# Routed-expert tiles of an FFN: list loads moved from SyncE's to ScalarE's DMA queue, and the weighting moved to the end of ScalarE's step

## The reference, cut to what matters

```python
y = cond_ref(x, ...)                          # 8192 tokens of 512, dense
shared = silu(xf @ sh_gate_w) * (xf @ sh_up_w) @ sh_down_w
topk_idx, w = _route(xf, router_w, e_bias)    # 8 of 64 experts for each token
order = argsort(topk_idx.reshape(-1)); tok = order // 8
g = ragged_dot(xf[tok], gate_w, group_sizes)  # 512 -> 256, by expert
u = ragged_dot(xf[tok], up_w, group_sizes)
o = ragged_dot(silu(g) * u, down_w, group_sizes) * w[order]
routed = zeros.at[tok].add(o)                 # out = x + shared + routed
```

## Time and profile before

| | us |
|---|---|
| median of 3 runs (4018.2 to 4027.15) | 4022.19 |
| the profiled execution, its own time | 3993.73 |
| span of the profiled execution | 3992.0 |
| routed part, from the first `e_sg` to the last | 2522.7 |
| PE busy in the span | 3867.9 (97%) |
| ACT busy in the span | 1444.0 (36%) |
| mean granted TensorE clock | 0.986 |

### The profile page before, as it was taken

One profiled execution on the slowest core, in us unless ns is written; L12 is line 12 of the kernel. 1 busy time (PEld: TensorE's weight loads), 2 busy tenths in 40 slices (PEclk: granted clock), 3 DMA queues, 4 the chain that ended last, 5 costly groups with the idle time before them and its releaser, 6 DMA issues.

```text
span 3992.0 us, 90448 instructions
## 1 busy us (share of the span) xinstructions
PE 3867.9 (97%) x19160; PEld 3180.6 (80%) x19161; DVE 1654.4 (41%) x3528; ACT 1444.0 (36%) x2807; POOL 1916.5 (48%) x1598
## 2 busy tenths in 40 slices
PE   6999999999999969999999999999999999999997
PEld 5888888888888758888888888888888888888875
DVE  4555555555555623333333333333333333333332
ACT  3222222222222223343343343434343443444443
POOL 1333333333333545555555555555554655555554
PEclk8999999999999979999999999999999999999998
DMA  5112211112211146676676676767677777777775
GB/s 177 43 49 59 60 47 43 43 55 64 53 43 43 33 102 111 113 140 115 111 141 113 125 128 113 137 117 137 118 140 134 120 137 138 122 140 140 141 139 112
DMA packets 372970, 408.94 MB, mean 102 GB/s; under 512 B 192457, under 2 KB 227409, under 8 KB 372881
## 3 DMA queue, kind: packets, MB, share of 16 engines
q0 software_dynamic: 135872, 280.60, 39.4%
q1 hardware_dynamic: 237010, 127.35, 12.5%
HBM read 228.83 MB, written 178.93 MB: 102 GB/s over the span
## 4 chain that ended last, share of the span: by engine, by line
PE 30%; DMA 19%; SPq 8%; issue 6%; POOLq 1%; POOL 0%; ACT 0%; DVE 0%; DVEq 0%; ACTq 0%
PE bank L1156 18%; DMA out_dram<-o_rows,list_s 11%; PE bank L1174 9%; DMA list_g<-slot_list 5%; SPq L1000 5%; PE bank L1147 2%; SPq L1035 2%; DMA raw_d<-in_L_ffn_down_w_dram 2%; PE bank L1165 2%; DMA x_rows<-y_rows,list_g 1%; SPq L1052 1%; POOLq L1000 0%; SPq L1054 0%; DMA list_s<-slot_list 0%; POOL x_rows L1093 0%
## 5 line engine op out<-in xcount | busy, mean ns | idle before, releaser
L1109 POOL DMA_INDIRECT out_dram<-o_rows,list_s x532 | 857.7, 1612 | 623.3 <-issue 313.5
L421 POOL DMA_INDIRECT slot_list<-ent,pos x512 | 498.8, 974 | 858.4 <-PE bank L445 718.4
L1315 DVE TENSOR_TENSOR e_hf<-bank,e_sg 128x256 f32<-128x256 f32 x532 | 225.9, 425 | 1619.1 <-ACT e_sg L1224 1205.5
L1156 PE MATMUL bank<-w_gu_h,x_h 128*128 x2128 | 836.5, 393 | 5.5 <-DVE w_dn_l L30 4.3
L1156 PE MATMUL bank<-w_gu_h,x_l 128*128 x2128 | 834.0, 392 | 0.0
L1156 PE MATMUL bank<-w_gu_l,x_h 128*128 x2128 | 829.3, 390 | 0.0
L1093 POOL DMA_INDIRECT x_rows<-y_rows,list_g x536 | 540.8, 1009 | 558.5 <-issue 317.2
L1224 ACT ACTIVATE e_sg<-bank 128x256 f32<-128x256 f32 x532 | 203.6, 383 | 955.0 <-PE bank L1156 951.0
L1238 ACT ACTIVATE o_rows<-bank,list_s 128x512 f32<-128x512 f32 x532 | 366.8, 690 | 495.1 <-PE bank L1174 417.1
L1156 PEld LDWEIGHTS bank<-w_gu_h,x_h 128*128 128x128 f32 x2128 | 400.4, 188 | 92.9 <-issue 9.3
L1174 PE MATMUL bank<-w_dn_h,e_h_h 128*128 x1064 | 472.2, 444 | 1.6 <-issue 0.5
(11 more groups left out here) (232 smaller groups left out, 5702.6 us busy)
## 6 DMA issues: line engine op xcount, KB each, us to landing
xin<-in_x_dram SPq DMA_DIRECT2D x16, 1024.0 KB, 7.2
y_rows<-yrow SPq DMA_DIRECT2D x64, 256.0 KB, 3.2
stage_d<-in_x_dram SPq DMA_DIRECT2D x16, 1024.0 KB, 7.2
out_dram<-stage_d SPq DMA_DIRECT2D x16, 1024.0 KB, 4.6
raw_gu<-in_L_ffn_gate_w_dram SPq DMA_DIRECT2D x29, 512.0 KB, 4.1
raw_gu<-in_L_ffn_up_w_dram SPq DMA_DIRECT2D x29, 512.0 KB, 6.5
raw_d<-in_L_ffn_down_w_dram SPq DMA_DIRECT2D x29, 512.0 KB, 7.6
list_g<-slot_list SPq DMA_DIRECT2D x536, 1.0 KB
```

The costliest lines, as they stand in the source:

```text
L421: nc.gpsimd.indirect_dma_start(slots, bass.IndirectOffsetOnAxis(ap=pos[v][:, t, k:k + 1], axis=0), ent[v][:, t, k, :], None).then_inc(scat ...
L1109: nc.gpsimd.indirect_dma_start(out, bass.IndirectOffsetOnAxis(ap=ls[u][:, 0:1].bitcast(U32), axis=0), og[u][:], None, compute_op=ALU.add). ...
L1156: last = nc.tensor.matmul(b_gu[u % 2][:], xp[a][:, u % 2, k, :], wgu[b][:, bass.ds(place, 1), k, :].rearrange("p a n -> p (a n)"), start=( ...
L1315: nc.vector.tensor_tensor(hf[:, u % 2, :], b_gu[u % 2][:, H:2 * H], sg[:, u % 2, :], ALU.mult).then_inc(dve_gu, 1)
```

## The change

SP's loop keeps only `weights(j)` for every tile, in order, without the waits for gathers and scatters. The loads of the lists are issued by ScalarE, through its own DMA queue: `list_gather(j+6)` behind `x_high(j+2)` in step j, and `list_scatter(j-2)` at the end of step j. `weigh(j-3)` moves from the start of ScalarE's step j to its end, ahead of `list_scatter`. The lists of the first six tiles are loaded by ScalarE at the start of the part, four of them before its first cast. At the end, the last two `list_scatter` stand ahead of the last three `weigh`.

```diff
@@ blk.sync
-                def step(g, u):
-                    n = g * UN + u
-                    known = isinstance(n, int)
-                    if not known or n >= UN:
-                        sp.wait_ge(x_ld[u], 16 * g)
...
-                    load_list(lg[u], lg_ld[u], n)
...
-                    if not known or n >= 3:
-                        weights(n - 3 + LEAD)
-                    if not known or n >= LAG_S:
...
-                            sp.wait_ge(added[(u - LAG_S) % UN], 16 * (g - (1 if u >= LAG_S - UN else 2)))
-                        load_list(ls[(u - LAG_S) % UN], ls_ld[(u - LAG_S) % UN], m)
...
+                for n in range(2 * UN):
+                    weights(n)
                 last_turn = field(sp, 0, 5, NTURN - 1)
+                with sp.Fori(2, NTURN + 1) as g:
                     with sp.If(last_turn >= g - 1):
                         for u in range(UN):
+                            weights(g * UN + u)
@@ blk.scalar
+                def load_list(dst, s, j):
+                    off = field(act, j, 0, LROWS - P)
+                    act.dma_start(dst[:], slots[bass.ds(off, P), :]).then_inc(s, 16)
+
+                def list_gather(j, u, g):
+                    if not isinstance(j, int) or j >= UN:
+                        act.wait_ge(x_ld[u], 16 * g)
+                        act.nop(nofuse=True)
+                    load_list(lg[u], lg_ld[u], j)
+
+                def list_scatter(j, u, g):
+                    if not isinstance(j, int) or j >= UN:
+                        act.wait_ge(added[u], 16 * g)
+                        act.nop(nofuse=True)
+                    load_list(ls[u], ls_ld[u], j)
...
-                    if not known or j >= 3:
-                        weigh(j - 3, (u - 3) % UN, g - 1 if u < 3 else g)
                     with act.If(turn.first(u + 2) > 0):
                         start_weights(j + 2, turn.order(u + 2))
                     silu(j, u)
                     x_high(j + 2, (u + 2) % UN)
+                    list_gather(j + 2 + UN, (u + 2) % UN, g + 2 if u >= UN - 2 else g + 1)
                     if not known or j >= 1:
                         h_high(j - 1, (u - 1) % UN)
                     with act.If(turn.first(u + 2) > 0):
                         end_weights(turn.order(u + 2))
+                    if not known or j >= 3:
+                        weigh(j - 3, (u - 3) % UN, g - 1 if u < 3 else g)
+                    if not known or j >= 2:
+                        list_scatter(j - 2, (u - 2) % UN, g - 1 if u < 2 else g)
...
-                weigh(UN * last_turn + UN - 3, UN - 3, last_turn)
                 h_high(end, UN - 1)
-                weigh(UN * last_turn + UN - 2, UN - 2, last_turn)
-                weigh(end, UN - 1, last_turn)
+                for u in range(UN - 2, UN):
+                    list_scatter(UN * last_turn + u, u, last_turn)
+                for u in range(UN - 3, UN):
+                    weigh(UN * last_turn + u, u, last_turn)
```

More of the change, by code:

```diff
@@ L994, in build @@
             assert MAXT % UN == 0 and NTURN > 2
-            LAG_S = 5
-            LEAD = 5
             def field(eng, j, f, top_val):
@@ L1055, in weights @@
                                      down_w[bass.ds(e, 1)].rearrange("e (k p) h -> p (e k) h", p=P)).then_inc(raw_d_ld, 16)
-                def step(g, u):
-                    n = g * UN + u
-                    known = isinstance(n, int)
-                    if not known or n >= UN:
-                        sp.wait_ge(x_ld[u], 16 * g)
-                    if known and n == 0:
-                        weights(0)
-                    load_list(lg[u], lg_ld[u], n)
-                    if known and n == 2:
-                        for early in range(1, LEAD):
-                            weights(early)
-                    if not known or n >= 3:
-                        weights(n - 3 + LEAD)
-                    if not known or n >= LAG_S:
-                        m = n - LAG_S
-                        if not known or m >= UN:
-                            sp.wait_ge(added[(u - LAG_S) % UN], 16 * (g - (1 if u >= LAG_S - UN else 2)))
-                        load_list(ls[(u - LAG_S) % UN], ls_ld[(u - LAG_S) % UN], m)
-                for n in range(3 * UN):
-                    step(n // UN, n % UN)
+                for n in range(2 * UN):
+                    weights(n)
                 last_turn = field(sp, 0, 5, NTURN - 1)
-                with sp.Fori(3, NTURN + 1) as g:
+                with sp.Fori(2, NTURN + 1) as g:
                     with sp.If(last_turn >= g - 1):
                         for u in range(UN):
[L1083 to L1086, removed]
+                            weights(g * UN + u)
             @blk.gpsimd
@@ L1272, in step @@
                         end_weights(turn.order(u + 2))
+                    if not known or j >= 3:
+                        weigh(j - 3, (u - 3) % UN, g - 1 if u < 3 else g)
+                    if not known or j >= 2:
+                        list_scatter(j - 2, (u - 2) % UN, g - 1 if u < 2 else g)
+                for u in range(UN):
+                    list_gather(u, u, 0)
                 act.wait_ge(words, 1)
@@ L1276, in _ @@
                 end_weights(0)
-                x_high(0, 0)
-                x_high(1, 1)
+                for u in range(2):
+                    x_high(u, u)
+                    list_gather(UN + u, u, 1)
                 turn = Turn(act, 0)
@@ L1294, in _ @@
                 end = UN * last_turn + UN - 1
-                weigh(UN * last_turn + UN - 3, UN - 3, last_turn)
                 h_high(end, UN - 1)
-                weigh(UN * last_turn + UN - 2, UN - 2, last_turn)
-                weigh(end, UN - 1, last_turn)
+                for u in range(UN - 2, UN):
+                    list_scatter(UN * last_turn + u, u, last_turn)
+                for u in range(UN - 3, UN):
+                    weigh(UN * last_turn + u, u, last_turn)
+                for u in range(2):
+                    act.wait_ge(lg_ld[u], 16 * last_turn + 48)
+                    act.nop(nofuse=True)
             @blk.vector
```

3 lines of the change are left out of this document (removed).

## The result

The changed kernel takes 4057.6 us (median of 5 runs, 4044.33 to 4061.05) against 4020.14 for the kernel before (5 runs): a ratio of 1.0078, 95% interval 1.0061 to 1.0094. Run once more on another chip it came to 4040.67 against 3997.91, 1.0095 (1.0066 to 1.0125). So the change costs 37 to 43 us. The forecast was 4004, with a range up to 4032.

The account below looks back on a forecast made before the run. TensorE, 97% busy, was taken as the bound, with 34.4 us lost in the routed part. Left or new 4 + 7 + 3 + 2 = 16, so 4022 - 18 = 4004 us; 8-in-10 range 3985 to 4032.

Parts of the forecast that it names:

- What bounds the kernel: Routed part: TensorE 97% busy, losing 34.4 us over the plain pace, 19.0 us of its waits for late gathered rows.
- Why moving the lists helps: Lists off SP no longer stand behind 1.5 MB of weights; waits for rows fall from 19 to 4 us.
- the queue doesn't matter: First rival: weights hold up gathers and lists from any queue; -9 to +1 us, within 0.2%; chance 0.2.
- Nothing lost, by 0.2 us: Expert changes: `weigh` behind the casts is done 4.3 to 4.8 us behind `e_sg`, against 5.0 wanted by `down`.
- The loop of `list_s` and `weigh`: `list_s` is issued behind one weighting and the next waits for it: 3 us lost in all, bounds 0 and 40.
- My third rival: The loop of `list_s` and `weigh` binds under weights: 25 to 30 us lost, result about 4022; chance 0.1.
- Change steps stall on `w_dn_l`: Expert changes: list loads on ScalarE delay the casts, 14 x 0.5, about 7 us; bounds 0 and about 40.
- A list load costs 1.2 us: ScalarE's sequencer: table read, register work and DMA take 1.2 us a load, twice in a step, 2.4 us.
- my second rival: ScalarE's change steps become the bound if loads cost 1.8 us: 5 to 30 us slower, near 4040; chance 0.12.
- Plain steps cost nothing: Steps without a change of expert: ScalarE's 1.5 us of slack covers the list loads, so no time is lost.
- Opening -2, end +2: Lists loaded first gain 2 us at the opening; two list loads ahead of late weightings lose 2 at the end.
- The sum: Whole routed part: 34.4 us lost now, 16 left or new, so 18 us gained; opening and end cancel.

Follow-up runs that it names:

- the square: Four cases against the kernel before: nothing moved 1.0000, lists moved to ScalarE 1.0003, weighting moved to the step's end 1.0126, both 1.0078 and 1.0095.

## Why the prediction was wrong, step by step

- **What bounds the kernel: right.** TensorE's waits near the changes, and rows that come late because their lists do. Where ScalarE issues `list_g` and the weighting is not late, `x_rows` goes from 19.0 to 0.6 us. (The price of the clock there was misread: a mean of 0.95 from levels of 0.5 and 1 is 10 us of the 100 at the lower level, not 5, and some 5 us lost, not 2.5. And there are 28 changes, not 27. Neither moves the forecast.)
- **Why moving the lists helps: half right.** The rival *the queue doesn't matter* falls by its outcome, since the rows' waits went; its premise holds for the lists, since one beside weights took as long on ScalarE's queue as on SP's (6.4 us and 5.8 to 6.8). The section of the Trainium skill quoted there, "DMA: Bandwidth & Descriptors", "Issuing engines are not separate DMA queues", agrees with these landing times. That the lists would be as late as now does not follow from it, since an earlier issue was what they needed. The other section, "Queues, rings and completion order", gives ScalarE rings of its own, and the profile shows them in use (`q10`, 154080 packets); no run here shows that they brought a list in sooner.
- **"Nothing lost, by 0.2 us" for `weigh` behind the casts: the step that failed.** Alone on the kernel before it costs 1.26%, about 50 us; without it the changed kernel has the time of the kernel before. Two things were wrong in it. The sum of 4.3 to 4.8 us against 5.0 took the step as starting on time. In the usual step it does: `weigh` starts 1.9 us behind `e_sg`, as forecast. At a pair of changes (3139 to 3149 us) the weighting was done 3.6 us behind `e_sg`, sooner than the sum said, but TensorE's `down` stood ready 2.4 us behind that `e_sg` and not 5.0: the cast and `e_sg` were themselves late, behind 3.57 us of `issue`. And I asked only when `down` wants the weighting. Behind it hang the scatter, GpSimd's next gather and, with lists on SP, SP's wait for the scatter: the 53.2 us of waits for rows. The sum for the gather, with 4.3 us spare, was worked out for a plain step.
- **The loop of `list_s` and `weigh`, 3 us in all (bounds 0 and 40): mis-sized.** Its landing under weights, feared at 6.3 us, was 6.4 at the median and 7.1 at most. Taking it off the late weighting gave back 29.8 us of the steps, and 0.4 to 0.6% of the time. The same loop with an early weighting costs almost nothing at 144 us of ScalarE's waits, so the price belongs to both edits together. My third rival had the mechanism and 25 to 30 us, though its own condition, two or three steps that lose 1 us each at 27 changes, makes 54 to 81.
- **Change steps stall on `w_dn_l`, 7 us: near.** The waits went from 4.3 to 13.1 in the changed kernel (8 or 10 forecast). But 25.6 and 24.8 us where the weighting goes first show what two loads cost the casts when nothing else is late ahead of them; the bound of 40 was the nearer end there.
- **A list load costs 1.2 us: right at the median (1.10 from its first row to the end of the issue), with a tail to 1.90.** The table read that the earlier trace rows has at 0.279 us lasts longer in many cases, now that it is made 1018 times. The read by itself, by line in the changed kernel, 1500 to 3900 us (minimum, median, longest, ns); that of 3139.8, ahead of the late cast above, took 934 ns:

```profile
L998 ACTq TENSOR_LOAD <-trow x1018: 51/284/1034, 1500.4 to 3898.3; - x170
```

  The longest loads are beyond the 1.6 us at which my second rival decides. Its time, 4040, is the nearest of all cases to the measured one; its sum stopped at 60 us where 27 changes of 3 us are 81. But the square shows that what decided was the weighting's place, which that rival and the main case both had at no cost.
- **Plain steps cost nothing: right**, five of them in 23.43 us; the 1.5 us of slack behind the claim was too much.
- **The sequencer runs ahead past a DMA: right.** `list_g` was issued at 3150.86 while the cast of 3149.72 was executing and `e_sg` (3151.11) was queued. The issue takes 0.34 us on ACTq, as forecast.
- **Opening -2, end +2:** -1.3 and +5.4. At the end `down` waits 3.01 us for `o_rows` (at 4033.75), since two loads in front of three weightings cost 2.22 us of `issue`, and the last scatters follow by landing.
- **The sum:** lost now 34.4, and left or new 16 forecast; measured 75.4. In the place of 4 us for `x_rows` stand 12.5; of 3 for the loop, 17.7 for `o_rows`; of 7 for the casts, 13.1 for `w_dn_l`; of 2 unnamed, 11.7 of `issue`. These make 55, a few of them at the end, behind the steps. Within the steps TensorE is idle for 51.9 us, and the rest is no wait: its busy time stands 23.4 us over the plain pace, where it stood 9.2 over it before.

What stays open: why the matmuls of the changed kernel are busy 14 us longer at a granted clock of 1.00; how the loss of the weighting's move divides, in the changed kernel, between the scatter-gather path and the direct wait of `down`, beyond what the two rows of waits (12.5 and 17.7 us) say; and why the dense part's end differs by up to 19 us between profiled executions. Neither was tried apart.

## What to carry to other kernels

An instruction that is moved back in a step must be priced by everything that hangs on its result, through the other engines and round again to the queue that feeds them, and at the crowded step, not at the plain one; "by 0.2 us" there is a stall. Moving a load to another engine lets it be issued earlier, ahead of what the first issuer waits for; the new queue by itself brought nothing in sooner here, and each load costs the new engine's sequencer a read, register work and the issue. Give it only the load that was late, behind the work that others wait for. When a change has two edits, run the four corners first: here one run of each edit alone told more than all waits.

## What the runs showed of the hardware

- ScalarE's read of a word from SBUF into a register takes 0.28 us at the median, but 0.93 us at 3139.8 and up to 1.03; GpSimd's and SP's reads of the same line show maxima of 1.01 and 1.16. The long ones have a place: in the changed kernel 225 of the 473 reads for `list_s` that are made while the weighting executes take over 0.5 us, and 9 of the 465 reads for `list_g` beside `x_h`. With both loads at the end of the step, 5 of 479 reads for `list_s` are that long. In the kernel before, none of the 19 reads of the table beside the weighting is, so the weighting alone doesn't make them long. What does wasn't tried.
- A DMA of 1 KB that was issued within 4 us behind an expert's last weight load took 5.8 to 6.8 us until its user ran when it went through the same queue as the weights, and 6.4 through another (medians; up to 8.9 and 7.1); away from weights 3.5 and 3.6.
- One kernel's medians on three chips were 3990.42, 3997.91 and 4024.81 us, 0.9% apart: larger than the change. Both traces from the slowest of the three, and the changed kernel's first, have one wait of 22 to 28 us for `remote` in the dense part; the other nine have none. Ratios on one chip, not times, carry the comparison.
